# Softplus of the step size: one ScalarE function straight from PSUM in place of Relu, Abs, Exp, Ln and an add, with dx and its transfers three slots earlier

## The reference

```python
x = silu(conv(x_in) + conv_b)                       # 4 taps along the tokens
delta = softplus(x @ W_delta_1 @ W_delta_2 + b_delta_2)
Bm, Cm = x @ W_B, x @ W_C
h = h * exp(delta * A) + (delta * x) * B            # per token, channel e and state n
y = sum over n of h * C
out = resid + ((y + x * W_D) * silu(skip)) @ W_out
```

## Time and profile before

| | us |
|---|---|
| median of three runs | 2518.38 (2516.23 to 2519.97) |
| the profiled execution's own time | 2516.55 |
| its span, first to last instruction | 2514.8 |
| first scan instruction | at 159.15 |
| first scan of step i = 7 | at 1137.74 |
| its slot 18 | at 1220.84 |
| its slot 31 | at 1276.15 |
| first scan of step i = 8 | at 1285.70 |

### The profile page before, as it was taken

One profiled execution on the slowest core, in us unless ns is written; L12 is line 12 of the kernel. 1 busy time (PEld: TensorE's weight loads), 2 busy tenths in 40 slices (PEclk: granted clock), 3 DMA queues, 4 the chain that ended last, 5 costly groups with the idle time before them and its releaser, 6 DMA issues. The chain is left out here.

```text
span 2514.8 us, 35818 instructions
## 1 busy us (share of the span) xinstructions
PE 2004.6 (80%) x11589; PEld 1611.3 (64%) x11589; DVE 1820.8 (72%) x3185; ACT 1860.7 (74%) x3716; POOL 1919.3 (76%) x1192
## 2 busy tenths in 40 slices
PE   3647776978888897888889797988978788787885
PEld 2446665767576775758667675867767576666652
DVE  3338776969687786968778786878778797688732
ACT  2467978697877878787877968788786978688631
POOL 0148887788887978788887977888887888899922
PEclk9869888989999898999989898998989999899996
DMA  3345555555464645556475555656465554655330
GB/s 125 102 159 170 175 169 190 192 182 189 143 224 162 205 154 190 188 166 209 130 235 177 181 171 159 214 165 218 139 207 175 169 192 129 215 164 194 122 108 17
DMA packets 239028, 425.94 MB, mean 169 GB/s; under 512 B 18878, under 2 KB 135162, under 8 KB 238842
## 3 DMA queue, kind: packets, MB, share of 16 engines
q1 hardware_dynamic: 238842, 423.65, 52.0%
HBM read 347.57 MB, written 76.02 MB: 168 GB/s over the span
## 5 line engine op out<-in xcount | busy, mean ns | idle before, releaser
L598 POOL TENSOR_TENSOR hc<-h,c_all 128x1024 f32<-128x1024 f32 x512 | 1208.5, 2366 | 303.1 <-DVE h L982 299.1
L982 DVE TENSOR_TENSOR_SCAN h<-operand,carry,bank 128x512 f32<-128x512 f32 x480 | 593.7, 1270 | 176.0 <-PE bank L1180 103.6
L1180 PE MATMUL bank<-ident,u_t 128*128 128x128 f32 x2560 | 439.9, 299 | 304.1 <-DVE h L982 296.3
L1185 PE MATMUL y_sum<-ident,hc 128*128 128x128 f32 x4096 | 641.4, 290 | 4.0 <-POOL hc L598 3.6
L1180 PEld LDWEIGHTS bank<-ident,u_t 128*128 128x128 f32 x2560 | 320.3, 153 | 455.4 <-ACT u_t L708 232.7
L708 ACT ACTIVATE u_t<-dx_t,b_t 128x256 f32<-128x256 f32 x1280 | 578.2, 505 | 0.0
L1185 PEld LDWEIGHTS y_sum<-ident,hc 128*128 128x128 f32 x4096 | 528.0, 152 | 54.3 <-issue 38.8
L582 POOL TENSOR_TENSOR operand<-dx_q,b_all 128x1024 f32<-128x1024 f32 x192 | 453.3, 2361 | 43.4 <-DMA dx_q<-dx_dram 43.4
L982 DVE TENSOR_TENSOR_SCAN h<-bank,carry,operand 128x512 f32<-128x512 f32 x288 | 360.4, 1274 | 133.7 <-ACT bank L689 107.8
L689 ACT ACTIVATE operand<-delta_q,neg_a 128x512 f32<-128x512 f32 x640 | 435.7, 716 | 0.2
L689 ACT ACTIVATE bank<-delta_q,neg_a 128x512 f32<-128x512 f32 x384 | 263.9, 687 | 109.5 <-DVE h L982 108.0
(11 more groups left out here) (129 smaller groups left out, 2329.3 us busy)
## 6 DMA issues: line engine op xcount, KB each, us to landing
c_all<-bc_dram SPq DMA_DIRECT2D x256, 512.0 KB, 4.1
b_all<-bc_dram SPq DMA_DIRECT2D x192, 256.0 KB, 5.3
win<-in_L_attn_W_in SPq DMA_DIRECT2D x64, 512.0 KB, 4.5
wskip<-in_L_attn_W_skip SPq DMA_DIRECT2D x64, 512.0 KB, 3.7
xd_dram<-hv SPq DMA_DIRECT2D x64, 256.0 KB, 4.2
delta_dram<-delta SPq DMA_DIRECT2D x32, 512.0 KB, 4.2
dx_dram<-dx SPq DMA_DIRECT2D x32, 512.0 KB, 6.8
delta_q<-delta_dram SPq DMA_DIRECT2D x32, 512.0 KB, 5.3
```

The lines of the kernel that those rows point to most:

```text
L598: nc.gpsimd.tensor_tensor(hc[:, number % 3], h[:, number % 3], c_all[:, j % 2, s % 2:s % 2 + 1].to_broadcast([P, 2, SPAN]), ALU.mult).then ...
L982: nc.vector.tensor_tensor_scan(h[:, number % 3, q], first, second, start, ALU.mult, ALU.add).then_inc(scan_done.sem, 1)
L1180: last = transpose(bank[:, q, b * P:(b + 1) * P], u_t[:, j % 2, b, q * P:(q + 1) * P], ident[:])
L1185: return matmul(to, lhsT=of, rhs=ident[:], is_transpose=True, start=start, stop=stop, skip_group_check=True)
```

## The change

ACT computes Softplus(z + b) from PSUM into `delta`, eight instructions of 128x256 in each step, at slots 21, 21, 23, 23, and signals `delta_ready` itself. Relu, Abs, Exp, Ln on ACT and the add on DVE go, with the semaphores `z_read`, `exp_z` and `ln_ready`. PE's products for pairs 2 and 3 move from slots 20 and 21 to slot 22, and wait for `delta_ready` of the pair that had the bank. POOL's products for dx move from slots 26 and 28 to 23 and 25, and wait themselves for the last store of `dx`. The stores of delta move from slots 26, 27 to 24, 26, those of dx from 28, 30 to 25, 27, and the load of the next stage's first quarter from 29 to 28.

```diff
@@ SP
-                                if s == 26 + eh:
+                                if s == 24 + 2 * eh:
                                     if v := due(sp, delta_ready, t, 2 * eh + 2):
...
-                                if s == 28 + 2 * eh:
+                                if s == 25 + 2 * eh:
                                     if v := due(sp, dx_ready, t, eh + 1):
...
-                        if s == 29 and i % 2:
+                        if s == 28 and i % 2:
                             load_quarter(t + 1, 0)
                             load_xd(t + 1, 0)
@@ POOL
-                                if s == 26 + 2 * eh:
+                                if s == 23 + 2 * eh:
                                     part = slice(eh * HALF, (eh + 1) * HALF)
                                     if v := due(pool, delta_ready, t, 2 * eh + 2):
                                         pool.wait_ge(delta_ready.sem, v)
+                                    if v := due(pool, dx_stored[eh], t - 1, 1):
+                                        pool.wait_ge(dx_stored[eh].sem, v)
@@ ACT
-                                if s == (19, 21, 21, 22)[p]:
+                                if s == (21, 21, 23, 23)[p]:
                                     if v := due(act, z_done, t, p + 1):
                                         act.wait_ge(z_done.sem, v)
...
                                     for e in range(2):
                                         et = 2 * p + e
-                                        v = pair_bank(p)[:, e * T:(e + 1) * T]
-                                        nc.scalar.activation(delta[:, et, :], v, ACT.Relu, bias=bdelta[:, et:et + 1])
-                                        last = nc.scalar.activation(dx[:, et, :], v, ACT.Abs,
-                                                                    bias=bdelta[:, et:et + 1])
-                                    last.then_inc(z_read.sem, 1)
+                                        last = nc.scalar.activation(delta[:, et, :], pair_bank(p)[:, e * T:(e + 1) * T],
+                                                                    ACT.Softplus, bias=bdelta[:, et:et + 1])
+                                    last.then_inc(delta_ready.sem, 1)
...
-                            if s == 23:
-                                if v := due(act, z_read, t, PAIRS):
-                                    act.wait_ge(z_read.sem, v)
-                                for eh in range(2):
-                                    part = dx[:, eh * HALF:(eh + 1) * HALF]
-                                    nc.scalar.activation(part, part, ACT.Exp, scale=-1.0).then_inc(exp_z.sem, 1)
-                            for p in range(PAIRS):
-                                if s == 24 + p // 2:
...
-                                    nc.scalar.activation(pair_bank(p)[:],
-                                                         dx[:, 2 * p:2 * p + 2].rearrange("p e t -> p (e t)"), ACT.Ln,
-                                                         bias=1.0).then_inc(ln_ready.sem, 1)
@@ DVE
-                            for p in range(PAIRS):
-                                if s == 25 + p // 2:
...
-                                    nc.vector.tensor_tensor(part, pair_bank(p)[:], part,
-                                                            ALU.add).then_inc(delta_ready.sem, 1)
@@ PE
-                                if s == (18, 20, 20, 21)[p]:
+                                if s == (18, 20, 22, 22)[p]:
...
-                                    if v := due(pe, z_read, t, p - 1):
-                                        pe.wait_ge(z_read.sem, v)
+                                    if v := due(pe, delta_ready, t, p - 1):
+                                        pe.wait_ge(delta_ready.sem, v)
```

More of the change, by code:

```diff
@@ L227, in build @@
         bt_turned, bt_ready = signal("bt_turned", "prep", 1), signal("bt_ready", "prep", 1)
-        z_done, z_read = signal("zd_done", "prep", PAIRS), signal("zd_read", "prep", PAIRS)
-        exp_z, ln_ready = signal("exp_z", "prep", 2), signal("ln_ready", "prep", PAIRS)
+        z_done = signal("zd_done", "prep", PAIRS)
         delta_ready, dx_ready = signal("delta_ready", "prep", PAIRS), signal("dx_ready", "prep", 2)
@@ L822, in _ @@
                                     last.then_inc(xd_ready.sem, 1)
-                                if s == (19, 21, 21, 22)[p]:
+                                if s == (21, 21, 23, 23)[p]:
                                     if v := due(act, z_done, t, p + 1):
                                         act.wait_ge(z_done.sem, v)
-                                    for stored in (delta_stored[p // 2], dx_stored[p // 2]):
-                                        if v := due(act, stored, t - 1, 1):
-                                            act.wait_ge(stored.sem, v)
+                                    if v := due(act, delta_stored[p // 2], t - 1, 1):
+                                        act.wait_ge(delta_stored[p // 2].sem, v)
                                     for e in range(2):
                                         et = 2 * p + e
-                                        v = pair_bank(p)[:, e * T:(e + 1) * T]
-                                        nc.scalar.activation(delta[:, et, :], v, ACT.Relu, bias=bdelta[:, et:et + 1])
-                                        last = nc.scalar.activation(dx[:, et, :], v, ACT.Abs,
-                                                                    bias=bdelta[:, et:et + 1])
-                                    last.then_inc(z_read.sem, 1)
+                                        last = nc.scalar.activation(delta[:, et, :], pair_bank(p)[:, e * T:(e + 1) * T],
+                                                                    ACT.Softplus, bias=bdelta[:, et:et + 1])
+                                    last.then_inc(delta_ready.sem, 1)
                             if s == 17:
@@ L1069, in _ @@
                                         op1=ALU.mult).then_inc(x_ready.sem, 1)
-                            for p in range(PAIRS):
-                                if s == 25 + p // 2:
-                                    if v := due(dve, ln_ready, t, p + 1):
-                                        dve.wait_ge(ln_ready.sem, v)
-                                    part = delta[:, 2 * p:2 * p + 2].rearrange("p e t -> p (e t)")
-                                    nc.vector.tensor_tensor(part, pair_bank(p)[:], part,
-                                                            ALU.add).then_inc(delta_ready.sem, 1)
                         if "mix" in jobs_now:
```

## The result

| | before | after |
|---|---|---|
| median of the runs side by side | 2517.3 us (4 runs) | 2432.2 us (2430.95 to 2434.21, 4 runs) |
| ratio | 1 | 0.9668, 95% interval 0.9653 to 0.9683 |
| span of the profiled execution | 2514.8 | 2431.3 |
| first scan instruction | 159.15 | 150.24 |

The change saves 85 us, 3.3%. The forecast was 2408 us, a gain of 110. The sign and the range held; the size was 25 us too large.

A forecast was written before the change was run, and what follows sets the result against it. ACT was taken to bound slots 18 to 30, and POOL once ACT is relieved. 60 + 18.5 + 15 + 16 = 109.5 us from 2516.55 gave 2407, 2408 for timed runs; 8-in-10 range 2372 to 2450.

The forecast's parts named there:

- slots 18 to 30, ten full steps: Steps 3 to 12: this stretch shortens by 6.0 us a step, 60 us in all.
- slots 18 to 30, the other steps: Steps 0, 1, 2 and 13: this stretch gains 3.5, 4.3, 5.2 and 5.5 us, 18.5 in all.
- slot 31 (load of `dx_q`): Odd steps' end: the load lands 8.7 us sooner, giving 2.1 us more at each of seven boundaries, 15 us.
- prologue: Steps -2 and -1, before the first scan: 7.0 and 9.2 us saved, sum 16.
- ACT's account: ACT in slots 18 to 30: 15.1 us removed, eight Softplus (2.9) and four switches (5.2) added; 53.9 becomes 46.9 us.
- rival that Softplus shares the exponential's table: ACT in slots 21 to 24: no table switches needed, and the load hides fully; 2364 us, chance 0.10.
- the one of two functions: Rival: Softplus worked in two functions with switches about each instruction, 3.3 us apiece; about 2640 us, chance 0.05.
- Nothing in it waits for ACT: POOL's queue from 1244.1 on: exponentials of slots 24 and 25 at old times, later ones up to 7 us sooner.
- the walk of POOL's queue: Slots 22 to 29: POOL packed from 1244.1 to 1274.4, so the next scan can start 6.7 us sooner.
- above 93%: Sign, slots 18 to 30 of step 7: POOL's busy share there, where it was 84%, with length 49 us.
- ACT stays the bound: Rival, slots 18 to 30: a switch costs 2.66 us, or Softplus about 1.0 above Relu; 2453 us, chance 0.17.
- 143: Sign, end of the prologue: the time in us at which the first scan was to start.

The follow-up runs named there:

- e1: The kernel after with Relu in Softplus's place on ACT, so no table switch stands in slots 21 to 24 (computes other numbers): 2396.2 us, ratio 0.953.
- e3: The kernel after with both dx products moved from POOL to DVE, in slot 24: 2435.2 us, ratio 0.969.
- e6: The kernel after with PE's products and Softplus at the slots from before the change, three visits to Softplus's table a step: 2487.6 us, ratio 0.990.
- e4: The kernel after with ACT's scaling of the router's output moved from slot 28 to 30, and POOL's gate sum to 30: 2434.6 us, ratio 0.968.
- e5: The kernel after with one visit to Softplus's table a step (slots 23 and 24), dx on POOL at 24 and 25: 2422.5 us, ratio 0.964.
- e8: The kernel after with one table visit, the router output's scaling moved later, and both dx products on DVE in slot 24: 2421.6 us, ratio 0.964.
- e7: The kernel after with stores of delta and dx and the next quarter's load at their old slots, dx products kept at 23 and 25: 2473.6 us, ratio 0.983.
- e2: The kernel after with Softplus kept, but dx products, stores and the next quarter's load at the slots of the kernel before: 2502.9 us, ratio 0.996.
- e11: e10 with the dx products on DVE, one half at slot 24 and one at 26: 2420.8 us, ratio 0.962.
- e10: The kernel after with one visit to Softplus's table a step and the next quarter's load at slot 27: 2407.0 us, ratio 0.956.

## Why the prediction was right, and where its size failed

Spans of the two profiled executions, cut at the scans, in us:

| term of the sum | predicted | measured |
|---|---|---|
| slots 18 to 30, ten full steps | 60 | 29.7 (2.97 a step) |
| slots 18 to 30, the other steps | 18.5 | 17.1 |
| slot 31 (load of `dx_q`) | 15 | 23.4 |
| prologue | 16 | 8.9 |
| slots 0 to 17, tail | 0 | 5.5, -1.2 |
| sum | 109.5 | 83.5 |

The sum came out nearer than its main term. The ten full steps gave half of what was forecast; slot 31 gave 8 us more than its 15, and slots 0 to 17 gave 5.5 that have no ground in the prediction. That these made up for part of it is luck.

**ACT's account: right.** Softplus at Relu's price, four loads of 1283 ns a step, ACT at 47.4 where 46.9 was forecast. The rival that Softplus shares the exponential's table fell by the 59 loads, the one of two functions by 0.36 us a piece.

**"Nothing in it waits for ACT": wrong, and here is the missing 30 us.** The step of the prediction that failed is the walk of POOL's queue: "with the switches in place the exponentials of slots 24 and 25 come at the old times", so that POOL is packed from 1244.1 on. POOL's products wait for DVE's scans, and the scans for the exponentials of slots 23 and 25, which stand behind a visit to Softplus. Scan 23 comes 22.2 us after slot 18's scan, where it had come 20.8 after it before, and scan 25 comes 31.5 after it, where it had come 28.9. I had moved the savings of slot 19 to slot 21: the Relu and Abs that went there only became a wait of ACT's for PE's transposes (1.33 us at 1183.60), and the scan of slot 22 starts at + 15.6 us in both kernels. POOL was busy for 87% of the stretch, not "above 93%". e1 takes the switches out and the stretch goes to the 49 us of the walk; e3 relieves POOL, and nothing moves; e6 adds switches and it grows. All three agree that between slots 22 and 25 the switches are on the path. At the end of the stretch it is ACT again and not POOL: DVE waits 2.48 us for the exponential behind the scalings, of which e4 takes off 1.4, and 0.4 for POOL. POOL becomes a bound where switches go: in e1 with 3.79 us of wait, in e5 with slot 28 at 4.4, which is 2.7 in e8 with POOL relieved.

The error has a form: I summed ACT's time over the stretch (46.9 of 49, so "not the bound") and didn't ask when in the stretch its exponentials come. An engine with 2 us of slack in 49 still stops its neighbour where 4.4 us lie in one piece.

**The rival "ACT stays the bound" (2453)** named the right engine and the wrong price. A switch costs 1.30 us here, from load to next start, as the earlier trace rows had it; the load at 1190.87 starts 0.02 us behind the exponential before it. The Trainium skill, "ScalarE: Activation LUTs", section "What ACT_TABLE_LOAD costs", gives 1283 ns for the load, and here the traces agree to the nanosecond; its drain of about 1380 ns on top is in none of them. A forecast by its 2.66 us would have been off by 21 us on the other side, less than this one was; that is chance, since placement, not the sum, makes a switch dear here.

**The load of `dx_q`: right in mechanism, larger than forecast.** 3.2 us at a full odd step and not 2.1, since the wait fell by more than the step's end moved. e7 shows how much hangs on it: with the stores and the load at the old slots 41 us of the gain go. POOL's waits on `dx_q` came to 20.4 us, where under 20 was named as the sign. The prediction costed this move by itself at 15; it didn't see that a shorter step without it makes the boundary worse (e2: 12.1 us against 9.6 before). Beside POOL's place for dx it is most of what the change is worth. Function alone 0.4%, with both moved 3.3%.

**The prologue: half.** The store of dx went out 11.1 us sooner (129.28 against 140.35), where 16 were forecast. Step -1 gave what its account had: from PE's product for z to this store it takes 9.1 us less, for 9.2. (The four terms of that account add up to 130.5, and not to the 131.1 that it states.) Step -2 was to give 7.0, and of this 1.9 were left when step -1 came to z: PE's product for z came at 120.95 against 122.89. ACT's copy of the earlier trace rows came 4.3 us sooner (81.86 against 86.19), although 1.4 had been lost before it, in a stretch (30 to 60 us) with a granted clock of 0.94 against 1.00. From the copy to z it then took 39.1 us instead of 36.7, at a clock of 0.78 against 0.84. Then the load of `dx_q` landed some 8.1 us after its issue (135.70) instead of 5.4, which took another 2.6; the stores and loads now go out in one burst (129 to 141), and that this slows the landing is a reading that no run divides. The stretch from 60 to 100 us, in the kernel before (first row), in the kernel after (second) and in e3 (third), whose first scan is at 141.1:

```profile
60.00:100.00 40.00, 22.76 (x78) 15.07 (x78) 8.50 (x24) 22.38 (x47) 7.89 (x13) 0.74 0.33 106
```

```profile
60.00:100.00 40.00, 27.68 (x85) 18.69 (x86) 10.20 (x35) 16.07 (x33) 7.95 (x13) 0.74 0.32 106
```

```profile
60.00:100.00 40.00, 28.00 (x110) 20.29 (x110) 16.07 (x50) 17.52 (x36) 3.25 (x11) 0.91 0.37 121
```

In equal busy time PE does 110 matmuls at a mean granted clock of 0.91 and 85 at 0.74, a larger part of them at 1.2 GHz. The first scans go with this clock: 139.7 to 141.1 in e6, e1 and e3 at 0.91; 144.1 and 144.6 in e8 and e5 at 0.85 and 0.86; 146.3 to 151.6 in the other changed kernels at 0.72 to 0.75. The kernel before has 0.74 as well, so the change didn't cost the clock there; it failed to win what e1, e3 and e6 won. What decides it was not settled. 143 lies between.

**Slots 0 to 17** gave 5.5 us that nobody forecast: 0.3 to 0.4 us a step over sixteen steps, less than what differs between the kernels' profiles in that stretch (81.7 to 83.4, where nothing was edited), so it isn't counted for the change.

## What to carry to other kernels

An engine that feeds a chain one step ahead is not judged by its busy share over a stretch: find the longest piece in which it gives the chain nothing, and set it against the slack at that point. Table switches are bought by the visit, so group the foreign function's work into one visit and put it where the next consumer already waits (the place is my inference from the two prices of e5 and e6, no run tests it alone). And a cheaper function pays only as far as its results also leave sooner: move the consumers, stores and loads with it, and then look at which queue's order holds them next (here one slot on SP, worth as much as a pair of switches).

## What the hardware showed that was not expected

VectorE and GpSimd hold each other up when both multiply float32 tensors in SBUF. In e11 (the first fence VectorE, the second GpSimd) the same product of 128x1024 on VectorE takes 2.71 us while GpSimd's products run, and the later of these takes 3.33 instead of 2.36; at slot 26 it takes 1.22 us, and an instruction of GpSimd's of two columns that takes 0.19 elsewhere lasts just as long as it, 1.27.

```profile
1190.44 2.71 DVE L1057 TENSOR_TENSOR dx<-delta,x 128x1024 f32<-128x1024 f32 x1 [0.76 <-ACT delta L731]
...
1202.07 1.22 DVE L1057 TENSOR_TENSOR dx<-delta,x 128x1024 f32<-128x1024 f32 x1
```

```profile
1189.71 2.36 POOL L597 TENSOR_TENSOR hc<-h,c_all 128x1024 f32<-128x1024 f32 x1 [0.59 <-DVE h L961]
1192.03 3.33 POOL L581 TENSOR_TENSOR operand<-dx_q,b_all 128x1024 f32<-128x1024 f32 x1
...
1202.07 1.27 POOL L555 TENSOR_TENSOR s_no<-s_no,s_ro 128x2 f32<-128x2 f32 x1
```

The Trainium skill, "GPSIMD Engine Reference", section "1. Specifications", says that the two share their SBUF interfaces and contend when VectorE has two SBUF inputs; these rows agree. In them it looks like taking turns and not like a slower pace. GpSimd's product that ran first keeps its 2.36 us and ends at 1192.07; VectorE's ends 1.1 us later, and GpSimd's next one is 1.0 us longer. No run was made to test that. What it cost differs: in e8 the two products stand in the chain and take 6.03 us, in e3 slot 24 grows by at most 0.6, and in e11 slot 24 is as long as in e10 (7.7), since VectorE idles there anyway. So it is a part of why dx on VectorE didn't pay in e8, and not the reason in e11, though VectorE's share of the span is the lower.
